# Attention kernel: one half value block per half step, the value copy between two exponentials, output tiles in the ring of score banks

## The reference, cut to what matters

```
xn = layernorm(x)                                  # x: 4 x 1024 x 256
q  = rotary(xn @ Wq) * 16**-0.5                    # 16 heads of 16
kv = rotary(xn @ Wkv)                              # keys and values are the same rows
attn = softmax(q @ kv.T)                           # per batch and head, 1024 x 1024
out  = attn @ kv
x + (out @ Wout + bout) + ffn(xn)                  # ffn: silu(gate) * up, int weights
```

## Time and profile before

| what | us |
|---|---|
| three timed executions | 888.66, 890.13, 1292.72 |
| their median | 890.13 |
| the profiled execution, its own time | 892.79 |
| its span in the trace | 890.9 |
| around the span | 1.9 |

### The profile page before, as it was taken

One profiled execution on the slowest core, in us unless ns is written; L12 is line 12 of the kernel. 1 busy time (PEld: TensorE's weight loads), 2 busy tenths in 40 slices (PEclk: granted clock), 3 DMA queues, 4 the chain that ended last, 5 costly groups with the idle time before them and its releaser, 6 DMA issues.

```text
span 890.9 us, 18505 instructions
## 1 busy us (share of the span) xinstructions
PE 841.5 (94%) x7018; PEld 316.9 (36%) x7018; DVE 767.5 (86%) x930; ACT 692.8 (78%) x1315; POOL 191.5 (21%) x411
## 2 busy tenths in 40 slices
PE   4999999999899999999999999999999999999997
PEld 2455655555422222222222223222222222322234
DVE  5888898888699999999999999988999999999902
ACT  4655445533689999999989999998998999999983
POOL 3533444534201000000211111111121111111120
PEclk9999999999899999999999999999999999999999
DMA  9012111011211111111111122211111122111222
GB/s 324 31 49 83 49 48 37 13 47 48 67 25 27 26 37 34 31 27 27 38 50 45 53 57 52 49 45 43 44 43 50 46 56 57 50 46 47 73 75 76
DMA packets 58493, 47.39 MB, mean 53 GB/s; under 512 B 18188, under 2 KB 48716, under 8 KB 58404
## 3 DMA queue, kind: packets, MB, share of 16 engines
q1 hardware_dynamic: 58404, 46.20, 18.4%
HBM read 28.57 MB, written 16.90 MB: 51 GB/s over the span
## 4 chain that ended last, share of the span: by engine, by line
PE 72%; DVE 12%; ACT 8%; issue 4%; DMA 1%; SPq 0%; POOL 0%; DVEq 0%; ACTq 0%
PE ps L695 23%; PE ps L675 12%; PE ps L712 11%; DVE negmax L1066 10%; PE ps L556 8%; ACT arena L921 7%; PE ps L534 7%; PE ps L584 4%; PE ps L720 3%; PE ps L573 1%; PE ps L616 1%; DMA x_all<-x_dram 1%; PE ps L520 1%; DVE stats L966 1%; ACT arena L935 1%
## 5 line engine op out<-in xcount | busy, mean ns | idle before, releaser
L1066 DVE TENSOR_REDUCE negmax<-ps 128x2 f32<-128x1024 f32 x512 | 595.0, 1218 | 46.3 <-PE ps L712 43.1
L921 ACT ACTIVATE arena<-ps 128x512 f32<-128x512 f32 x1024 | 555.6, 597 | 56.2 <-PE ps L675 34.8
L695 PE MATMUL ps<-arena 128*32 128x256 f32 (+1 forms) x3664 | 316.7, 418 | 0.3 <-ACT arena L921 0.2
L675 PE MATMUL ps<-qs,ks 51*128 51x512 f16 x1024 | 199.4, 385 | 24.6 <-ACT arena L921 23.5
L712 PE MATMUL ps<-ks,qs 48*128 48x512 f16 x976 | 190.7, 387 | 3.6 <-DVE negmax L1066 3.6
L695 PEld LDWEIGHTS ps<-arena 128*32 128x32 f32 x3664 | 72.4, 108 | 115.1 <-issue 100.6
L712 PEld LDWEIGHTS ps<-ks,qs 48*128 48x128 f16 x976 | 47.0, 93 | 172.7 <-issue 133.8
L851 ACT ACTIVATE side<-ps 128x512 f32<-128x512 f32 x48 | 28.7, 598 | 95.0 <-PE ps L556 94.4
L675 PEld LDWEIGHTS ps<-qs,ks 51*128 51x128 f16 x1024 | 51.0, 93 | 136.9 <-ACT arena L921 107.3
L556 PE MATMUL ps<-arena,side 128*128 128x512 f16 x384 | 88.8, 380 | 0.3 <-DVE side L1014 0.3
L1202 POOL TENSOR_TENSOR side<-side 128x512 f16<-128x512 f32 x48 | 57.2, 1192 | 52.7 <-ACT side L857 52.6
(11 more groups left out here) (87 smaller groups left out, 481.9 us busy)
## 6 DMA issues: line engine op xcount, KB each, us to landing
parts_d<-arena SPq DMA_DIRECT2D x64, 128.0 KB
x_all<-x_dram SPq DMA_DIRECT2D x8, 512.0 KB, 8.6
qs<-parts_d SPq DMA_DIRECT2D x64, 64.0 KB, 1.9
ks<-parts_d SPq DMA_DIRECT2D x64, 64.0 KB, 1.9
o_d<-arena SPq DMA_DIRECT2D x124, 32.0 KB
arena<-o_d SPq DMA_DIRECT2D x24, 128.0 KB
arena<-inv_d SPq DMA_DIRECT2D x48, 64.0 KB
out_dram<-arena SPq DMA_DIRECT2D x24, 128.0 KB, 1.8
```

The source lines that it names most:

```text
L675: mm = pe.matmul(ps[:, score_bank(ls, 2 * half + a), :], ks[ring][top:top + ROWS, kt * P:(kt + 1) * P], qs[ring][top:top + ROWS, half * CH ...
L695: mm = pe.matmul(ps[32 * j:32 * j + 32, 7, cols], vstage[pl % 2][:, j % 2, kt, :], probs[PER_STEP * (kt % PBUF) + j][:, cols], start=(kt = ...
L921: act.activation(probs[PER_STEP * (kt % PBUF) + j], ps[:, score_bank(ls, j), :], ACT.Exp).then_inc(exp_done, 1)
L1066: dve.tensor_reduce(negmax[pl % 2][:, h, :, kt], ps[:, bank:bank + 2, :], AX.X, ALU.max, negate=True).then_inc(max_done, 1)
```

## The change

Every pair now has the same table: the halves of the value blocks go to slots 4 to 19, one in each slot, so slots 0 to 3 of the next pair take the last four. Only the last pair has whole blocks, in slots 14, 15 and after the loop. The maxima are always last in their slot. `copy_o` moves from behind the first exponential of step 1 to behind its third, since the last half block is now issued in slot 3. The tile projection of slot 3 no longer goes to bank 7 but takes a place of its own in the ring of three score banks, between the places of slots 3 and 4, and `copy_tile` moves to behind the fourth exponential of step 1. The place shifts the banks of the scores after it, so the bank is now worked out from a running number over all pairs. A new function `free` gives the wait for a ring place; `scores` calls it once for each of its two places, where it had one wait on the exponentials before.

```diff
-PER_PAIR = PER_STEP * STEPS + 1
+TILE_INDEX = 2 * (TILE_SLOT + 1)
 WHOLE = None
-TILE_VALUES = {...}
-PLAIN_VALUES = {...}
+VALUES = {PBUF + n: divmod(n, 2) for n in range(2 * STEPS)}
+LAST_VALUES = {n: VALUES[n] for n in range(PBUF, 14)} | {14: (5, WHOLE), 15: (6, WHOLE), 16: (7, WHOLE)}
...
+        def with_tile(p):
+            return p >= LAG
+
+        def pair_base(p):
+            return (PER_STEP * STEPS + 1) * p + max(p - LAG, 0)
+
+        def place(p, kt, j):
+            n = PER_STEP * kt + j
+            return pair_base(p) + n + (n >= TILE_INDEX) * with_tile(p) + (n >= TURN_INDEX) * (p + 1 < PAIRS)
...
+        def score_bank(n):
+            return 4 + n % 3
...
+            def free(p, n):
+                if n < 0:
+                    return
+                if n < pair_base(p):
+                    p -= 1
+                if p + 1 < PAIRS and n == turn_place(p):
+                    pe.wait_ge(mrows_done, p + 2)
+                elif with_tile(p) and n == tile_place(p):
+                    pe.wait_ge(wout_copied, p - LAG + 1)
+                else:
+                    n -= pair_base(p)
+                    n -= with_tile(p) and n > TILE_INDEX
+                    n -= p + 1 < PAIRS and n > TURN_INDEX
+                    pe.wait_ge(exp_done, PER_STEP * STEPS * p + n + 1)
...
-                last = ring_index(ls, 2 * half + 1) - 3
-                if turned_here and TURN_INDEX in (last - 1, last):
-                    pe.wait_ge(mrows_done, p + 2)
-                tiles = last + 1 - (last >= TURN_INDEX)
-                if not isinstance(turn, int) or turn or ls // STEPS or tiles > 0:
-                    pe.wait_ge(exp_done, PER_STEP * STEPS * p + tiles)
+                for a in range(2):
+                    free(p, place(p, kt, 2 * half + a) - 3)
...
-                    if tile:
-                        pe.wait_ge(wout_copied, tile[0] + 1)
...
-                    long = (tile and slot == TILE_SLOT) or (block and block[1] is WHOLE)
-                    if more and long:
-                        maxima(turn, m, half)
-                    if tile and slot == TILE_SLOT:
-                        pe.wait_ge(o_copied, p)
-                        project_tile(*tile, 7)
+                    block, of, pair = (LAST_VALUES if p + 1 == PAIRS else VALUES).get(slot), p, pl
+                    if block is None and p:
+                        block, of, pair = VALUES.get(slot + 2 * STEPS), p - 1, pl - 1
                     if block:
-                        values(of, pair, *block, tile)
+                        values(of, pair, *block)
...
+                    if slot == TILE_SLOT and with_tile(p):
+                        free(p, tile_place(p) - 3)
+                        project_tile(p - LAG, (p - LAG) % 2, score_bank(tile_place(p)))
-                    if more and not long:
+                    if more:
                         maxima(turn, m, half)
...
-            for slot in range(2 * STEPS, 2 * STEPS + 3):
-                values(PAIRS - 1, RING - 1, *PLAIN_VALUES[slot])
+            values(PAIRS - 1, RING - 1, *LAST_VALUES[2 * STEPS])
...
-                    if j == 0 and kt == COPY_O_AT and not (isinstance(p, int) and p == 0):
-                        copy_o(p - 1, ls // STEPS - 1, turn)
...
-                    if tile and j == 0 and kt == (TILE_SLOT + 1) // 2:
-                        copy_tile(*tile)
+                    if j == 2 and kt == COPY_O_AT and p:
+                        copy_o(p - 1, pl - 1, turn)
+                    if j + 1 == PER_STEP and kt == COPY_O_AT and with_tile(p):
+                        copy_tile(p - LAG, (p - LAG) % 2, score_bank(tile_place(p)))
...
-                act.activation(res[k], ps[:, 7, 0:DIM], ACT.Copy).then_inc(wout_copied, 1)
+                act.activation(res[k], ps[:, bank, 0:DIM], ACT.Copy).then_inc(wout_copied, 1)
```

More of the change, by code:

```diff
@@ L654, in _, with scores @@
                 turn_qk(c)
-            def scores(turn, ls, half, turned_here=True):
+            def free(p, n):
[12 more added lines that the diff above has]
+                    pe.wait_ge(exp_done, PER_STEP * STEPS * p + n + 1)
+            def scores(turn, ls, half):
                 p = turn * RING + ls // STEPS
@@ L665, in scores, with values @@
                     pe.wait_ge(m_in[ring], 32 * (turn + ls // (RING * STEPS) + 1))
-                last = ring_index(ls, 2 * half + 1) - 3
-                if turned_here and TURN_INDEX in (last - 1, last):
-                    pe.wait_ge(mrows_done, p + 2)
-                tiles = last + 1 - (last >= TURN_INDEX)
-                if not isinstance(turn, int) or turn or ls // STEPS or tiles > 0:
-                    pe.wait_ge(exp_done, PER_STEP * STEPS * p + tiles)
+                for a in range(2):
+                    free(p, place(p, kt, 2 * half + a) - 3)
                 for a in range(2):
                     top = HEAD_ROWS * a
-                    mm = pe.matmul(ps[:, score_bank(ls, 2 * half + a), :], ks[ring][top:top + ROWS, kt * P:(kt + 1) * P],
+                    mm = pe.matmul(ps[:, score_bank(place(p, kt, 2 * half + a)), :], ks[ring][top:top + ROWS, kt * P:(kt + 1) * P],
                                    qs[ring][top:top + ROWS, half * CHUNK:(half + 1) * CHUNK], start=True, stop=True)
                 mm.then_inc(scores_done, 1)
-            def values(p, pl, kt, part, tile=None):
+            def values(p, pl, kt, part):
                 if kt == 0:
@@ L736, in project_back, with step @@
                           start=False, stop=False)
-            def step(turn, ls, last_turn=False, tile=None):
+            def step(turn, ls, last_turn=False):
                 pl = ls // STEPS
@@ L745, in step @@
                     slot = 2 * (ls % STEPS) + half
[L746 to L750, removed]
-                    long = (tile and slot == TILE_SLOT) or (block and block[1] is WHOLE)
-                    if more and long:
-                        maxima(turn, m, half)
-                    if tile and slot == TILE_SLOT:
-                        pe.wait_ge(o_copied, p)
-                        project_tile(*tile, 7)
+                    scores(turn, ls, half)
+                    block, of, pair = (LAST_VALUES if p + 1 == PAIRS else VALUES).get(slot), p, pl
+                    if block is None and p:
+                        block, of, pair = VALUES.get(slot + 2 * STEPS), p - 1, pl - 1
                     if block:
-                        values(of, pair, *block, tile)
-                    if last_turn and pl + 1 == RING:
+                        values(of, pair, *block)
+                    if p + 1 == PAIRS:
                         if slot == 0:
@@ L768, in step @@
                             project_front(FRONT_AT[slot])
-                    if slot == 2 * T_AT and (not last_turn or pl + 1 < RING):
-                        turn_max(p + 1, pl + 1, (exp_done, PER_STEP * (STEPS * p + T_AT)), turn_bank)
-                    if more and not long:
+                    if slot == 2 * T_AT and p + 1 < PAIRS:
+                        turn_max(p + 1, pl + 1, (exp_done, PER_STEP * (STEPS * p + T_AT)), score_bank(turn_place(p)))
+                    if slot == TILE_SLOT and with_tile(p):
+                        free(p, tile_place(p) - 3)
+                        project_tile(p - LAG, (p - LAG) % 2, score_bank(tile_place(p)))
+                    if more:
                         maxima(turn, m, half)
@@ L784, in _ @@
                     step(i, ls)
-            for i in range(TURNS - TILES_FROM):
+            for i in range(TILES_FROM, TURNS):
                 for ls in range(FIRST, FIRST + RING * STEPS):
-                    step(i + TILES_FROM, ls, tile=loop_tile(i, ls))
+                    step(i, ls)
             for ls in range(FIRST, RING * STEPS):
-                n = LAST - LAG + ls // STEPS - FIRST_SLOT
-                step(TURNS, ls, True, (n, n % 2))
-            for slot in range(2 * STEPS, 2 * STEPS + 3):
-                values(PAIRS - 1, RING - 1, *PLAIN_VALUES[slot])
+                step(TURNS, ls, True)
+            values(PAIRS - 1, RING - 1, *LAST_VALUES[2 * STEPS])
             pe.wait_ge(back_divided, CPB)
@@ L865, in high_qk, with rows @@
                     act.activation(parts[g][:, 0, :], bank_turn(g), ACT.Copy).then_inc(hi_done, 1)
-            def rows(p, slot, turn, bank=turn_bank):
+            def rows(p, slot, turn, bank):
                 act.wait_ge(mturned, p + 1)
@@ L908, in _, with exps @@
             act.activation(warm[:, :], epsb[:, :], ACT.Exp)
-            def exps(turn, ls, tile=None, last_turn=False):
-                p = turn * RING + ls // STEPS
+            def exps(turn, ls):
+                pl = ls // STEPS
+                p = turn * RING + pl
                 kt = ls % STEPS
@@ L916, in exps @@
                 for j in range(PER_STEP):
-                    if j == 0 and not (isinstance(s, int) and s < PBUF):
+                    if j == 0 and s >= PBUF:
```

(20 more changed lines are left out.)

19 lines of the change are left out of this document (4 added, 15 removed).

## The result

The changed kernel takes 912.48 us (median of 4 runs, 910.92 to 913.20) against 891.18 for the kernel before beside it: ratio 1.0244, 95% interval 1.0218 to 1.027. The ratio leaves out one disturbed run of the kernel before, 1292.72 us. Slower, outside the range of 872 to 893. The profiled execution has a span of 909.1 us.

The account below looks back on a forecast made before the run. Bound: the loop from scores through exponential to next scores, and TensorE's own work, both near 1.13 us a slot. Plain pairs -4.0, tile pairs -6.7, last pair +0.5 give -10.2: 890.13 to 879.9 us, range 872 to 893.

Parts of the forecast that it names:

- Two waits ahead of the scores: TensorE's queue ahead of the scores: two waits on the exponentials' semaphore are joined into the later one, cost 0.
- Separate waits: Rival, chance 0.17: unjoined waits ahead of scores in 449 more slots cost 0.06 to 0.09 us each, giving 909 us.
- Whole blocks to halves: Slots 14, 12 and 5: halves replace whole value blocks, saving 0.40 us a plain pair, 0.44 in slots 12-15 of tile pairs.
- The copy between two exponentials: Slots 3 and 4 of plain pairs: the moved value copy costs the same, 2.66 us for 2.65, change taken as 0.
- The tile in the ring: Slots 3 to 5 of the 21 tile pairs: 4.54 us for 4.42, so 0.12 lost a pair.
- The last pair: Last pair: two half blocks more in the loop, between 0 and 1.1 us more, 0.5 taken.
- The count of separate waits if joined: Sign at the scores' ring waits: near 85 instructions of their own if joined, near 500 if not.
- The sum: Whole kernel: -4.0 for plain pairs, -6.7 for tile pairs, +0.5 for the last pair, -10.2 us in all.
- VectorE takes over: Rival, chance 0.15: VectorE falls behind, the maxima matmuls hold TensorE and the saving is lost, 890 us.
- The copy hides: Rival, chance 0.06: ScalarE's idle time absorbs the value copy's delay, saving 12.4 us more, 867.5 us.
- Wrong would be the whole reckoning if quiet slots changed from 1.13: Sign: quiet slots, mean 1.13 us from scores to scores, must stay so, or the whole reckoning is wrong.

Follow-up runs that it names:

- joined: The changed kernel with only the later wait kept where both score waits are on the exponentials' semaphore: 879.1 us, ratio 0.986 to the kernel before.
- the second experiment: The changed kernel with both waits kept, but the wait for the later exponential first in the program: 874.76 us, ratio 0.9806 to the kernel before.
- the best kernel: The joined kernel with the wait that the loop hangs on first in `scores` and `exps`: 864.47 us, ratio 0.9692 to the kernel before.

## Why the prediction was wrong, point by point

**The step that failed** is "Two waits ahead of the scores", where it says "I take 0, since joining loses nothing". The two waits were not joined. The count is 511, not 85, and the later wait, on which the loop hangs, stood alone. This was the rival "Separate waits", at a chance of 0.17: "the later one, on which the loop hangs, stands alone in nearly every slot" is what the trace shows, and its time of 909 lies 3.5 from the measured 912.48. Its price was right: 0.05 to 0.09 a slot was given, 0.05 in odd and 0.09 in even slots is measured, 1.00 in a pair. 31 pairs make 31 us, where 31 less 2 were reckoned: slot 4 of a plain pair was covered in part only and still paid 0.04, and slot 12 paid 0.10. Of the 32.3 between after and joined in the profiled executions, pair 0 holds 2.4 (20.83 and 18.48) and the last pair 0.5.

The argument "Against: a program builder can drop the earlier wait" had no row behind it. The earlier trace rows had one behind the other side: 63 scores with two waits did have an instruction of their own. Those rows showed what a second wait becomes; I tied it to "two different semaphores", which they did not show. What also was missed is the order: the price was seen only where the wait that comes last in time stands alone, and the program's order decides that.

By the rule of the Trainium skill (Advanced Engine Details and Errata, section Network/Comms) the prediction had an estimate of 22 to 45 us for these waits. The measured 33.4 lies inside, and the 0.05 to 0.09 a slot near its 50 to 100 ns: the trace agrees, for a wait that the loop hangs on. For one that is met already the second experiment shows no cost.

**What was right**, by the joined kernel:

- *Whole blocks to halves.* Slot 14 forecast at 1.14: 1.14. Slots 12 to 15 forecast at 5.10 in both kinds: 5.10 to 5.12, down from 5.50 and 5.54.
- *The copy between two exponentials.* Slots 3 and 4 forecast at 2.66: 1.12 + 1.54 = 2.66. That the value block might be held by the copy was named as an end of the range. It is held, a little; joined, slots 3 and 4 of pair 8:

```profile
387.77 0.39 PE L692 MATMUL ps<-qs,ks 51*128 51x512 f16 x2
...
388.89 0.38 PE L692 MATMUL ps<-qs,ks 51*128 51x512 f16 x2
389.49 0.64 PE L710 MATMUL ps<-arena 128*32 128x256 f32 x8 [0.22 <-issue]
...
390.43 0.39 PE L692 MATMUL ps<-qs,ks 51*128 51x512 f16 x2
```

  The block starts 1.72 behind the scores of slot 3 (forecast: 1.63) and delays nothing that the copy did not delay already.
- *The tile in the ring.* Slot 3 forecast at 2.20: 2.18. Slot 4 forecast at 0.49 + 0.66 + 0.07 = 1.22: 1.22. The pair forecast at about 19.8: 19.78.
- *The last pair.* 0.5 was taken, 0.7 came: from its first scores to the end 38.3 for 37.7.
- *The count of separate waits if joined.* 85, as said.
- *The sum.* -10.2 from 890.13, 879.9, against 879.1 measured. That is closer than the steps deserve, and partly luck. Against the median beside it (891.37) joined gains 12.3. In the profiled executions the parts are -3.5 (9 plain pairs), -7.0 (21 tile pairs) and +0.7 (last), which is -9.8; the front part gave 0.9 by itself, and pair 0 gave 3.4, most of it with the clock and not with the change (last section). Since the executions of one kernel differ in this by as much, the agreement within 1 us can't be read as a test of the terms; the slots can.

**The other rivals.** *VectorE takes over* fell: VectorE kept up with pairs of 18.64 and 19.27, and moving the maxima ahead of the tile gained nothing. *The copy hides* fell: slot 4 is 1.54 joined and 1.54 in the best kernel, so its 0.4 a pair is still spent.

"Wrong would be the whole reckoning if quiet slots changed from 1.13": they changed, to 1.23 and 1.17. The sum of the other terms held, and this term, put at 0, is where the forecast broke.

## What to carry to other kernels

Where an instruction has more than one wait, put the one that comes last in time first in the program, and leave out a wait that another on the same semaphore implies; in a loop of 1.1 us this alone moved 33 to 38 us of 912. When a trace shows stray wait instructions, find out what makes a wait stand alone before you add a second one, and price it at both ends. And a slowdown in one loop isn't a price times a count: it uncovers waits elsewhere, so the same edit cost 33.4 us in one kernel and 16.6 in another.

## What the runs showed that I had not expected

**First in the program rides, the rest stand alone.** An instruction of them is 51 ns on TensorE and 17 on ScalarE, where it is met. On the loop a slot pays 0.05 to 0.09 on TensorE, and 0.02 to 0.06 on ScalarE; a standing wait that is already met costs nothing that shows, nor did the one of slot 0 whose instruction had started early.

**TensorE's clock in the first pair.** The attention part begins with few value blocks, and in some executions the granted clock falls there. A stretch ahead of the fall and the stretch 239 to 245 us in the trace of the kernel before (PE, PEld, DVE, ACT, POOL, clock):

```profile
235.50:238.50 3.00, 1.77 (x14) 0.48 (x18) 3.00 (x3) 3.00 (x7) 0.24 (x2) 1.00 0.43 111
239.00:245.00 6.00, 6.00 (x42) 1.07 (x40) 3.68 (x3) 3.61 (x7) 0.00 (x0) 0.50 0.01 3
```

Ahead of the fall TensorE was busy 1.77 of 3.00 us. Then it was busy all 6.00 us, at 0.50 of full speed, 1.2 GHz, with 42 matmuls. The joined kernel, 7 us at the same place:

```profile
238.00:245.00 7.00, 7.00 (x76) 2.21 (x76) 6.64 (x7) 6.76 (x14) 0.57 (x3) 1.00 0.01 2
```

Full clock, 2.4 GHz, with 76. Pair 0 took 21.87 us in the profiled execution of before, 20.83 after, 18.3 to 18.5 in three kernels and 19.7 to 21.5 in the other five. The granted clock of 234 to 256 us is 1.00 in exactly the three short ones, and 0.84 or 0.92 in the other seven. So up to 3.5 us lie in this one pair and go with the clock, as large as the whole term for plain pairs. The fall comes and goes without an edit: the mean granted clock of the kernel before, over 15 executions beside the last experiments, is 0.995 to 1.0; the two above 0.998 took 887.92 and 888.07 us, the others 889.37 to 894.24. Whether an edit makes the fall likelier stays open. In the profiled execution of the best kernel the pair takes 19.68, above the 18.3 of others.
